# A residual attention and FFN block on one core: the attention's small PSUM evacuations move from ScalarE to VectorE

## The reference

```python
s = einsum('btd,dm->btm', xn, Win) + bin_          # 512 -> 64
h = relu(s[..., None] * W1 + b1)                   # 64 x 16
g = einsum('btmh,mh->btm', h, W2) + b2
ffn = einsum('btm,md->btd', g, Wout) + bout        # 64 -> 512

q, k, v = (xn2 @ Wq.T + bq) * s4, xn2 @ Wk.T * s4, xn2 @ Wv.T + bv   # xn2: a second layer norm; 16 heads of 32
for it in range(3):
    ql, kl, vl = q[:, :, :16] @ Wlq.T + blq, k[:, :, :16] @ Wlk.T + blk, v[:, :, :16] @ Wlv.T + blv
    a = softmax(ln(ql) * tscale @ (ln(kl)).T * sm_scale) @ vl
    q, k, v = q + a, kl, vl
attention = a_selected @ Wo.T + bo
```

## Time and profile before

| | |
|---|---|
| time, median of 3 runs | 329.03 us (328.23 to 329.45) |
| time of the profiled execution | 329.03 us |
| its span, first to last instruction | 327.2 us |
| PE busy | 296.1 us, 90% |
| DVE busy | 257.5 us, 79% |
| ACT busy | 234.0 us, 72% |
| POOL busy | 237.0 us, 72% |
| moved by DMA | 87.80 MB, mean 268 GB/s |

### The profile page before, as it was taken

The page is one execution under the profiler, slowest core; times in us unless marked ns, Lnnn a source line. Parts: engine busy times, 40 slices in busy tenths (PEclk is TensorE's granted clock), DMA queues, the critical chain, the costliest instruction groups (busy, mean ns, idle before and its releaser), DMA issues.

```text
span 327.2 us, 5159 instructions
## 1 busy us (share of the span) xinstructions
PE 296.1 (90%) x1804; PEld 132.0 (40%) x1804; DVE 257.5 (79%) x400; ACT 234.0 (72%) x308; POOL 237.0 (72%) x209
## 2 busy tenths in 40 slices
PE   3797499989989999999999999999999999999683
PEld 3543364544433544344443434343434243432220
DVE  1818965589599787897879999989897989976435
ACT  1516755675896869879698668888878788886830
POOL 8523992771992989659892966978969496989930
PEclk9999989999999999999999999999999999999999
DMA  7999929995529899698979999899999997425458
GB/s 237 300 373 405 256 23 337 403 212 193 182 94 331 230 310 317 180 343 248 334 198 314 314 297 310 249 351 270 332 309 354 334 373 245 184 115 219 134 184 339
DMA packets 50569, 87.80 MB, mean 268 GB/s; under 512 B 6360, under 2 KB 35184, under 8 KB 46448
## 3 DMA queue, kind: packets, MB, share of 16 engines
q1 hardware_dynamic: 46400, 65.96, 66.1%
q10 hardware_dynamic: 3504, 21.37, 18.0%
q0 software_dynamic: 640, 0.16, 0.8%
HBM read 53.77 MB, written 33.69 MB: 267 GB/s over the span
## 4 chain that ended last, share of the span: by engine, by line
PE 60%; DVE 25%; DMA 6%; issue 5%; ACT 2%; SPq 0%; ACTq 0%; DVEq 0%
PE op L548 13%; PE s L489 13%; PE g L526 12%; PE T L465 7%; DVE stats L957 6%; DVE x L930 6%; PE rep L510 3%; DMA out_dram<-x 3%; DMA x<-in_L_attn_x_dram 3%; PE op L347 2%; DVE xqT L940 2%; ACT H L701 1%; PE A L320 1%; DVE SL L951 1%; PE A L418 1%
## 5 line engine op out<-in xcount | busy, mean ns | idle before, releaser
L1064 POOL TENSOR_TENSOR x<-x,bias_row 128x512 f32<-128x512 f32 x128 | 162.7, 1313 | 2.5 <-DVE bias_row L812 2.5
L701 ACT ACTIVATE H<-rep,b1c,w1c 128x1024 f32<-128x1024 f32 x128 | 146.8, 1220 | 17.7 <-PE rep L510 13.2
L930 DVE TENSOR_TENSOR x<-x,op 128x1024 f32<-128x1024 f32 x62 | 75.1, 1211 | 29.0 <-PE op L548 28.9
L957 DVE BATCH_NORM_STATS2 stats<-x 128x6 f32<-128x512 f32 x128 | 80.7, 678 | 7.8 <-DMA x<-in_L_attn_x_dram 7.6
L548 PE MATMUL op<-wout,G 64*128 64x512 f32 x248 | 68.4, 628 | 5.2 <-DVE x L930 5.2
L1048 POOL TENSOR_TENSOR rstd<-veps,nhalf 128x8 f32<-128x8 f32 x16 | 26.7, 1671 | 51.7 <-DVE veps L967 51.6
L526 PE MATMUL g<-H,w2s 128*32 128x512 f32 x512 | 63.0, 600 | 0.4 <-ACT H L701 0.4
L489 PE MATMUL s<-xT,win 128*64 128x512 f32 x128 | 59.9, 612 | 0.9 <-ACT xqT L676 0.8
L676 ACT ACTIVATE xT<-T 128x512 f32<-128x512 f32 x60 | 36.4, 606 | 31.0 <-PE T L465 27.3
L489 PE MATMUL s<-xqT,winq 128*64 128x512 f32 x112 | 51.1, 598 | 0.0
L465 PE MATMUL T<-ident,x 128*128 128x128 f32 x256 | 43.5, 295 | 6.0 <-ACT xT L676 2.9
(11 more groups left out here) (170 smaller groups left out, 291.3 us busy)
## 6 DMA issues: line engine op xcount, KB each, us to landing
out_dram<-x SPq DMA_DIRECT2D x30, 1024.0 KB, 6.1
x<-in_L_attn_x_dram ACTq DMA_DIRECT2D x10, 2048.0 KB, 11.8
xq<-in_L_attn_x_dram SPq DMA_DIRECT2D x112, 128.0 KB, 7.3
x<-in_L_attn_x_dram SPq DMA_DIRECT2D x12, 1024.0 KB, 11.5
out_dram<-x SPq DMA_DIRECT2D x4, 512.0 KB, 3.3
x<-in_L_attn_Wq_dram SPq DMA_DIRECT2D x1, 1024.0 KB, 17.6
x<-in_L_attn_Wk_dram SPq DMA_DIRECT2D x1, 1024.0 KB, 19.8
x<-in_L_attn_Wv_dram SPq DMA_DIRECT2D x1, 1024.0 KB, 17.2
```

The costliest lines, as they stand in the source:

```text
L701: act.activation(Hr[half][k % len(Hr[half])][:, :], rep_ps[:, :], ACT.Relu, bias=b1c[:, half, k:k + 1], scale=w1c[:, half, k:k + 1]).then_ ...
L930: dve.tensor_tensor(both, both, sum_banks(n, j)[:, :].rearrange("p (h d) -> p h d", h=2), ALU.add).then_inc(add_done, 1)
L957: dve.bn_stats(stats[:, j, :], x_sb[m][:, j * D:(j + 1) * D]).then_inc(bn_done, 1)
L1064: pool.tensor_tensor(x_sb[m][:, c], x_sb[m][:, c], bias_row[:, :], ALU.add).then_inc(xc_done, 1)
```

## The change

Four of the attention's steps in each round go from ACT to DVE. ACT made them of several small operations with a per-partition scale or bias; DVE makes `qk`, `Vbd` and `kbd` of one operation each with a broadcast second input, and `kT` and `vT` of one each. The semaphores `norm_made` and `kbd_made` go, since norm, kbd and the scaling of q now follow each other on DVE. All four tables of places are new; the three rounds and the last step, which ran from body 3 to body 9, now end in body 8.

```diff
@@ pe_attention, lg
                 pe.wait_ge(qs_made, it + 1)
-                pe.wait_ge(kbd_made, it + 1)
@@ act_attention, each round
-                act.wait_ge(lin_ps, it + 1)
-                for i in range(2):
-                    ins = act.activation(qk[:, i, :], A_ps[:, i * CR:(i + 1) * CR], ACT.Identity, bias=bqk[:, i:i + 1])
-                ins.then_inc(lin_made, 1)
...
-                act.wait_ge(kv_ps, it + 1)
-                act.activation(kT[:, :], A_ps[:, 0:CR], ACT.Identity, bias=blkv[:, 0:1])
-                act.activation(vT[:, :, :, :], chunks(A_ps[:, CR:2 * CR]).unsqueeze(2).to_broadcast([P, DC, 2, RW]),
-                               ACT.Identity, bias=blkv[:, 1:2]).then_inc(kv_made, 1)
...
-                act.wait_ge(vt_ps, it + 1)
-                act.wait_ge(masks_made, 1)
-                for a in range(2):
-                    ins = act.activation(Vbd[:, :, a, :], A_ps[:, :].rearrange("p (g a d) -> p g a d", a=2, d=HD)[:, :, a, :],
-                                         ACT.Identity, scale=half2[:, a:a + 1])
-                ins.then_inc(vbd_made, 1)
...
-                act.wait_ge(norm_made, it + 1)
-                for h in range(hpc):
-                    ins = act.activation(kbd[:, :, h, :], chunks(qk[:, 1, :]), ACT.Identity, scale=hmask[:, h:h + 1])
-                ins.then_inc(kbd_made, 1)
@@ dve_attention, each round
+                dve.wait_ge(lin_ps, it + 1)
+                dve.tensor_tensor(qk[:, :, :], A_ps[:, :].rearrange("p (a c) -> p a c", a=2),
+                                  bqk[:, :].unsqueeze(2).to_broadcast([P, 2, CR]), ALU.add).then_inc(lin_made, 1)
+                yield next(AT_DVE)
+                dve.wait_ge(kv_ps, it + 1)
+                dve.tensor_scalar(kT[:, :], A_ps[:, 0:CR], blkv[:, 0:1], None, ALU.add)
+                dve.tensor_scalar(vT[:, :, :, :], chunks(A_ps[:, CR:2 * CR]).unsqueeze(2).to_broadcast([P, DC, 2, RW]),
+                                  blkv[:, 1:2], None, ALU.add).then_inc(kv_made, 1)
+                yield next(AT_DVE)
+                dve.wait_ge(vt_ps, it + 1)
+                dve.tensor_tensor(Vbd[:, :, :, :], A_ps[:, :].rearrange("p (g a d) -> p g a d", a=2, d=HD),
+                                  half2[:, :].unsqueeze(1).unsqueeze(3).to_broadcast([P, H2, 2, HD]), ALU.mult).then_inc(vbd_made, 1)
+                yield next(AT_DVE)
                 dve.wait_ge(rw_ps, it + 1)
-                dve.tensor_tensor(flat(qk[:, :, :]), flat(qk[:, :, :]), A_ps[:, :], ALU.mult).then_inc(norm_made, 1)
-                yield next(AT_DVE)
-                dve.wait_ge(norm_made, it + 1)
+                v = tick(dve.tensor_tensor(flat(qk[:, :, :]), flat(qk[:, :, :]), A_ps[:, :], ALU.mult))
+                yield next(AT_DVE)
+                dve.wait_ge(dve_own, v)
+                dve.tensor_tensor(kbd, chunks(qk[:, 1, :]).unsqueeze(2).to_broadcast([P, DC, hpc, RW]),
+                                  hmask[:, :].unsqueeze(1).unsqueeze(3).to_broadcast([P, DC, hpc, RW]), ALU.mult)
@@ the first lines of the table of DVE
-            -32, -32, -32, 34, 36, 40, 41, 41, 41, 41, 48, 48, 48, 64, 69, 69, 73, 77, 77, 77, 80, 96, 98, 100, 102,
+            -32, -32, -32, 34, 34, 36, 39, 39, 39, 39, 41, 48, 48, 48, 69, 69, 71, 74, 74, 74, 79, 80, 96, 98, 99,
```

More of the change, by code:

```diff
@@ L180, in residual_block @@
                              "at_ps", "at_made", "ai_ps", "ai_made"))
-        norm_made, kbd_made = sem("norm_made"), sem("kbd_made")
         dif_made, abs_made, dif_ps, sel_made, att_ps, att_made, acc_done = (
@@ L191, in residual_block @@
         AT_PE = iter((
-            -32, 47, 47, 47, 66, 66, 67, 67, 67, 67, 68, 68, 68, 70, 70, 73, 74, 75, 75, 75, 77, 79, 98, 101, 104,
-            106, 108, 110, 111, 132, 137, 143, 161, 164, 166, 169, 171, 175, 196, 207, 225, 228, 230, 233, 235, 239,
-            260, 271, 289, 294, 298,))
+            -32, 45, 45, 45, 47, 47, 66, 66, 67, 67, 68, 68, 68, 70, 70, 73, 73, 74, 74, 74, 75, 77, 79, 98, 101,
+            103, 105, 107, 109, 111, 132, 141, 143, 162, 165, 167, 169, 173, 175, 201, 203, 205, 207, 225, 226, 232,
+            237, 258, 261, 265, 268,))
         AT_ACT = iter((
-            46, 46, 65, 65, 65, 69, 69, 71, 72, 72, 72, 104, 104, 106, 108, 128, 128, 132, 138, 142, 163, 164, 165,
-            167, 170, 170, 192, 200, 206, 227, 228, 229, 231, 234, 234, 256, 264, 270, 290, 296,))
+            43, 43, 46, 65, 65, 69, 69, 70, 72, 72, 72, 103, 104, 108, 134, 139, 161, 166, 168, 194, 199, 204, 224,
+            228, 238, 257, 262, 266,))
         AT_DVE = iter((
-            -32, -32, -32, 34, 36, 40, 41, 41, 41, 41, 48, 48, 48, 64, 69, 69, 73, 77, 77, 77, 80, 96, 98, 100, 102,
-            130, 130, 134, 135, 140, 141, 161, 192, 193, 194, 195, 200, 201, 225, 256, 257, 258, 259, 264, 265, 289,
-            290, 292,))
[3 rows of a table added]
         AT_POOL = iter((
-            8, 8, 103, 128, 135, 167, 199, 231, 263,))
+            8, 8, 103, 103, 133, 167, 195, 226, 231,))
         def reach(steps, n, place):
@@ L622, in act_attention @@
             act.activation(vn, A_ps[:, 0:D // 2], ACT.Copy).then_inc(vn_made, 1)
-            blkv = rep[:, 3 * HD + 1:3 * HD + 3]
             for it in range(ROUNDS):
-                yield next(AT_ACT)
-                act.wait_ge(lin_ps, it + 1)
-                for i in range(2):
-                    ins = act.activation(qk[:, i, :], A_ps[:, i * CR:(i + 1) * CR], ACT.Identity, bias=bqk[:, i:i + 1])
-                ins.then_inc(lin_made, 1)
                 yield next(AT_ACT)
@@ L865, in dve_attention @@
             dve.tensor_copy(bqk[:, :], A_ps[:, 0:2]).then_inc(bqk_made, 1)
+            blkv = rep[:, 3 * HD + 1:3 * HD + 3]
             v = tick(dve.tensor_scalar(hmask[:, :], block4[:, ::HD], rep[:, 3 * HD + 4:3 * HD + 5], None, ALU.mult))
```

## The result

The changed kernel takes 332.91 us (330.25 to 337.53, 4 runs) where the kernel before took 328.63 beside it: a ratio of 1.0121, with a 95% interval of 1.0079 to 1.0166. Run again on the chip of eight of the experiments it takes 332.76 (ratio 1.0163 [1.0127, 1.0199]). The medians of this document count every execution, while the ratios and their intervals leave out those that took over 1.5% more than the fastest of their kernel. The forecast was 328.2 us, from 325.0 to 332.8. The profiled execution took 333.36 us, 4.3 more than the one before, around a span of 331.5.

The account below looks back on a forecast made before the run. PE was taken as the bound in the attention bodies, with DVE now level with it. The sum was 329.03 - 3.1 (early chain) + 0.9 + 0.7 (DVE's queue) + 0.7 (store wait) = 328.2 us, range 325.0 to 332.8.

Parts of the forecast that it names:

- part 2: DVE's in-order queue in the attention bodies: a loss of 0.9 us in bodies 3 and 4, 0.7 in bodies 5 to 9.
- Part 1: Operations moved from ACT to DVE: 11.1 us more DVE work over three rounds, plus 0.9 for kbd's possible contention with POOL.
- Body 3 comes out level: Body 3, the first with attention: no loss; bodies 3 and 4 together lose 0.9 us (0 to 2).
- The walk: Bodies 3 to 9 stepped through with estimated durations: bodies 5 to 9 sum to 95.1 us, against 94.4 before after adjustment.
- 1 + 0.4 + 0.3 us: Body 4: PE waits about 1 us for add 0, some 0.4 for add 1 and 0.3 for SL.
- Part 3: Ahead of the attention: earlier layer norm and weight copies start product_qk at 43.4 us, not 46.48, gaining 3.1 us (1.0 to 4.5).
- loads allow it: Block 3's first half, issued at about 46 us, landed 6.5 us later and is wanted near 57 us.
- Part 4: Behind the attention: one more fast body, n = 9, adds one wait behind a store, 0.7 us (0 to 1.5).
- DVE becomes the bound: Rival, chance 0.30: add j stands behind kbd, kT and vT in bodies 4, 5, 7 and 8; 333.1 us.
- Its own sign: DVE over 95% busy from the start of body 3 to the end of body 8, with PE holes that end at an add.
- Two thirds of its extra: The milder form of that rival, with two thirds of its added 4.9 us: 331.6 us.
- Slower: Whole kernel: a measured time above 330.7 us, chance 0.30.

Follow-up runs that it names:

- POOL's short adds: POOL's bias add done on only 8 of the 512 columns of each row: in the changed kernel 328.62 us, in the kernel before 322.80 us.

## Why the prediction failed

The step that failed is part 2, DVE's queue. It gave bodies 3 to 9 a loss of 0.9 + 0.7 = 1.6 us, and they lost 11.3: DVE's results that PE waits for came late in bodies 3, 4 and 8, and the holes of bodies 3 to 8 sum to 12.2 us where the forecast had about 6.3 and set 9 as its limit.

**Part 1, the moved operations: right in size.** The forecast was 11.1 us and 0.9 more for kbd. The moved steps took about 12.5 us, and DVE as a whole gained 13.8; kbd took 1.22, 1.23 and 2.29 us, within its bounds. But the contention with POOL was looked for at kbd alone. Three operations that did not change engine met it in the changed kernel: the masks (3.56 us, 1.96 before), prob (median 1.55, with POOL's short adds 0.68) and wq_it (1.23 us, 0.69 before, and 0.23 with short adds). For the masks and prob, which have two inputs in SBUF, this agrees with the Trainium skill (SBUF — State Buffer, section "SBUF: two separate sides"), as do the masks at 0.67 us when one input lies in PSUM.

**Part 2, DVE's queue: the failed step.** "Body 3 comes out level": it lost 4.7 us. The walk had the masks short and did not ask who waits for them; the low clock behind the hole is some 1.6 of it (PE busy 21.01 us, and 19.42 for the same body at a clock of 1.00). Body 4 was to lose 0.9 and lost 1.8, or 0.6 in the execution whose clock stayed up. The waits that the walk names there, 1 + 0.4 + 0.3 us, are also only 0.35 more than the 1.35 of before, so its 0.9 does not follow from them. It had norm, kbd, wq_it and qs at 2.8 + 1.5 us, and they took 4.4: the durations were right. What it missed is that PE's logits wait for this chain: it said that s_product hides kbd and qs in round 1 and sum_h in round 2, and gave round 0 only the wait of add 0. In round 2 the cover did not suffice either; PE waits 0.99 us for qs. Bodies 5 to 9 were to take 95.1 us and took 99.7; nearly all of the difference is body 8, walked as 20.2 and measured 24.63. I had spread the last round's and the last step's work over bodies 6 to 8 by its sum. The loss of 0.7 (-1 to +4) is 4.9 us there.

**Part 3, the early chain: right where it looked, wrong about what keeps it.** Product_qk came at 39.34 us against a forecast of 43.4; with the 2.9 us of the run added back it is 42.2. PE's hole shrank to 2.65 us, as forecast, and the clock stayed at 1.00, so the copies came 1.5 us apart and not 2.0, and body 2 gave 4.0 us, near the upper bound of 4.5. A run with the old early places whose body 2 began at 25.35 took 33.22 us for it, so this part is the change's. The clock is not sure, though: with the same places and as long a hole, body 2 had 0.94 and took 30.1 to 30.7 us in three of the other profiles. But "from there to 66 us PE has no hole, so the gain is kept" did not look behind 66 us, and "loads allow it" looked at block 3's first half and not at its quads: the masks and, in some executions, the quads hold body 3 up, and the early places alone bring 327.43 us against 327.37.

**Part 4** was a miss on the cheap side: no extra store wait; the two that exist are 0.6 and 0.4 us long, before 0.7 each.

**The rivals.** "DVE becomes the bound" gave 333.1 us and the right sign, but that it came within 0.2 us is luck. Its own sign, DVE over 95% busy from body 3 to body 8, was not met: it is 88% there, and over 95% in bodies 6 and 8 alone. Its mechanism, adds standing behind kbd, kT and vT, is a minor part: of the 12.2 us of holes only some 1.7 end at an add. (Two thirds of its extra make 331.5 us, not 331.6.) "Slower" had a chance of 0.30; a body-by-body walk with the masks' readers in it would have made it likelier.

## What to carry to other kernels

That a queue is on average 84% busy says nothing of the step that stands ahead of what the bound engine waits for: walk each wait, also those of steps that only move by a place. Where a gain passes several waits in a row (here the copies, the masks, the loads), the first lever alone can bring nothing; ask what ends the wait next and when its data land. When steps change engine, give the operation that everyone waits for to the engine that is free at that moment. An operation with a second input in SBUF, beside a busy POOL, is shorter here when it reads its first from PSUM rather than from a copy in SBUF; that saved 2.9 us of DVE time, but alone no time of the kernel that is clear of the noise.
